# Cross-attention and routed feed-forward on one core: fewer TensorE waits, a split subtraction moved ahead, the last V projection one tile later, and P before rstd in four tiles

## What is computed

```python
x = x + attention(layernorm(x), ctx, ctx, Wq, Wk, Wv, Wo, padding_mask, attention_mask)
x = x + tiled_ffn(layernorm(x), tile_sigs, W, b)
# attention: 16 heads of 32; scores / sqrt(32), masked to -inf, softmax, NaN rows to 0
# tiled_ffn: each position s goes through one of 8 experts:
#   idx = argmax(pe @ sign(tile_sigs).T);  y[b, s] = x[b, s] @ W[idx[s]].T + b[idx[s]]
```

## Time and profile before

| what | value |
|---|---|
| median of three runs | 868.12 us (867.82 to 868.56) |
| the profiled execution's own time | 870.69 us |
| its span, first to last instruction | 868.9 us |
| mean granted TensorE clock | 0.982 of full speed |
| busy share: PE, PE weight loads, DVE, ACT, POOL | 96%, 77%, 81%, 47%, 73% |
| tile loop of the attention | from about 43 us to about 655 us of the span |
| expert stage, PE without a pause | from about 677 us to about 860 us |

### The profile page before, as it was taken

One profiled execution on the slowest core, in us unless ns is written; L12 is line 12 of the kernel. 1 busy time (PEld: TensorE's weight loads), 2 busy tenths in 40 slices (PEclk: granted clock), 3 DMA queues, 4 the chain that ended last, 5 costly groups with the idle time before them and its releaser, 6 DMA issues. The chain is left out here.

```text
span 868.9 us, 25184 instructions
## 1 busy us (share of the span) xinstructions
PE 832.7 (96%) x9583; PEld 669.5 (77%) x9584; DVE 707.6 (81%) x1026; ACT 405.3 (47%) x650; POOL 630.3 (73%) x825
## 2 busy tenths in 40 slices
PE   8999999999999999999999999999883999999996
PEld 6777778778778787887888788777663788888885
DVE  4998898888888888888888888888868877777774
ACT  5545556454654655465555545554555222222221
POOL 3688778786878768776877877686566677777774
PEclk9999999999999999999999999999986999999998
DMA  9522432524253343424344252432578899999992
GB/s 336 197 77 60 152 118 93 159 78 146 75 169 103 112 141 94 150 74 152 100 130 137 84 163 74 136 101 75 174 252 265 251 287 289 300 283 298 294 283 80
DMA packets 123153, 142.08 MB, mean 164 GB/s; under 512 B 16128, under 2 KB 89376, under 8 KB 120992
## 3 DMA queue, kind: packets, MB, share of 16 engines
q1 hardware_dynamic: 108656, 99.45, 36.9%
q0 software_dynamic: 11360, 35.66, 12.7%
q10 hardware_dynamic: 3024, 5.45, 2.0%
HBM read 90.18 MB, written 51.90 MB: 164 GB/s over the span
## 5 line engine op out<-in xcount | busy, mean ns | idle before, releaser
L1818 PE MATMUL banks<-wf_hl,x_hi 128*128 x560 | 139.1, 391 | 1.9 <-DVE wf_hl L356 1.1
L1110 POOL TENSOR_TENSOR s<-s,row 128x1024 f32<-128x1024 f32 x64 | 121.7, 1902 | 3.5 <-DVE row L1360 3.5
L1818 PEld LDWEIGHTS banks<-wf_hl,x_hi 128*128 128x128 f32 x560 | 105.3, 188 | 24.4 <-issue 2.7
L1759 ACT CAST x_hi<-x2t 128x512 fp32r<-128x512 f32 x70 | 43.5, 621 | 148.7 <-PE banks L1818 136.4
L1505 PE MATMUL banks<-wo_hi,ot_hi 128*128 128x512 f32 x256 | 107.8, 421 | 0.0
L1505 PE MATMUL banks<-xt_hi,wq_hi 128*128 128x512 f32 x256 | 105.1, 411 | 0.4 <-ACT vd L1192 0.3
L1086 POOL TENSOR_SCALAR y_mom<-y_mom 128x1 f32<-128x1 f32 x64 | 16.0, 251 | 120.7 <-DVE y_mom L1381 119.5
L1505 PE MATMUL banks<-wo_lo,ot_hi 128*128 128x512 f32 x256 | 101.6, 397 | 0.0
L1505 PE MATMUL banks<-wo_hi,ot_lo 128*128 128x512 f32 x256 | 101.5, 397 | 0.0
L1505 PE MATMUL banks<-xt_hi,wq_lo 128*128 128x512 f32 x256 | 100.5, 392 | 0.0
L1070 POOL TENSOR_TENSOR xt_lo<-xt_raw,xt_hi 128x512 fp32r<-128x512 f32 x64 | 94.4, 1504 | 7.5 <-ACT xt_hi L1177 7.5
(11 more groups left out here) (132 smaller groups left out, 1863.2 us busy)
## 6 DMA issues: line engine op xcount, KB each, us to landing
xq<-x_scratch SPq DMA_DIRECT2D x280, 64.0 KB
xt_raw<-in_x_t SPq DMA_DIRECT2D x16, 1024.0 KB, 6.7
x<-in_x SPq DMA_DIRECT2D x64, 256.0 KB, 3.5
y_scratch<-y_biased SPq DMA_DIRECT2D x64, 256.0 KB, 2.2
x_scratch<-y_normal SPq DMA_DIRECT2D x64, 256.0 KB, 2.9
wf_hl<-in_wf ACTq DMA_DIRECT2D x5, 1024.0 KB, 5.3
ctx_raw<-in_ctx_t SPq DMA_DIRECT2D x32, 128.0 KB, 3.5
wf_hl<-in_wf SPq DMA_DIRECT2D x3, 1024.0 KB, 7.7
```

Source lines behind the costliest of these rows:

```text
L1110: pool.tensor_tensor(p, p, h.row[:, t % h.c, 3, :].unsqueeze(2).broadcast_to([P, H, BK]), ALU.mult)\
L1818: return pe.matmul(pA[:, r % 2, :], rows[:, r % 2, c * P:(c + 1) * P], w, start=first, stop=last)
```

## The change

It has four parts.

1. Waits on TensorE are left out where an earlier wait of the same engine already covers them: in `scores` the ones on `s_drained` (but for t = 1) and `kt_copied`; in `transpose_p` the two on `p_copied` (but for the last tile); in `weigh_v` the one on `ot_lo_ready` and the two on `p_copied` (but for the last two tiles).
2. On POOL, the first piece of wo's low part is put ahead of `normalise_p(0)`, the other three directly behind it, and the wait for `shifted` is dropped.
3. V of the last group is projected in tile 59 and not in tile 58, on TensorE, in ACT's `v_copy` and in the order of the fills.
4. In tiles 59 to 62 POOL does `normalise_p(t + 1)` before `rstd(t + 2)` and not behind it.

```diff
+    def values_at(self, g):
+        return None if g >= self.groups else self.c * g - (1 if g == self.groups - 1 else 2)
...
-            if q == 2 and g + 1 < self.groups:
+            if t == self.values_at(g + 1):
                 names.append(("V", g + 1))
...
+            pool.wait_ge(w_hi_ready["o"], 1)
+            low_of_o(0)
             normalise_p(0)
-            pool.wait_ge(shifted, 2)
-            pool.wait_ge(w_hi_ready["o"], 1)
-            for c in range(KC):
-                ins = pool.tensor_tensor(w_lo["o"][:, c, :], wo_raw[:, c * DM:(c + 1) * DM],
-                                         w_hi["o"][:, c, :].bitcast(F32), ALU.subtract)
+            for c in range(1, KC):
+                ins = low_of_o(c)
             ins.then_inc(w_lo_ready["o"], 1)
...
+                    late = h.tiles - 6 < t < h.tiles - 1
                     if t >= 2:
                         y_rstd(t - 2)
+                    if late:
+                        normalise_p(t + 1)
                     if t + 2 < h.tiles:
                         rstd(t + 2)
...
-                    if t + 1 < h.tiles:
+                    if t + 1 < h.tiles and not late:
                         normalise_p(t + 1)
...
-                    if q == 2 and g + 1 < h.groups:
+                    if t == h.values_at(g + 1):
                         v_copy(g + 1)
...
             def scores(t):
                 g, q = divmod(t, h.c)
-                wait(pe, s_drained, t)
+                if t == 1:
+                    pe.wait_ge(s_drained, t)
                 wait(pe, p_copied, 2 * (t - 1))
                 if q == 0:
-                    pe.wait_ge(kt_copied, g + 1)
                     pe.wait_ge(q_copied, KC * g + KC)
...
                 for b in range(2):
-                    wait(pe, p_copied, 2 * (t - 1) + b + 1)
+                    if t + 1 >= h.tiles:
+                        pe.wait_ge(p_copied, 2 * (t - 1) + b + 1)
...
             def weigh_v(t):
                 g, q = divmod(t, h.c)
-                wait(pe, ot_lo_ready, t)
                 if q == 0:
                     pe.wait_ge(v_copied, g + 1)
                 for c in range(2):
-                    pe.wait_ge(p_copied, 2 * t + c + 1)
+                    if not h.has_scores(t):
+                        pe.wait_ge(p_copied, 2 * t + c + 1)
...
-                    if q == 2 and g + 1 < h.groups:
+                    if t == h.values_at(g + 1):
                         project_v(g + 1)
```

3 lines of the change are left out of this document (added).

## The result

The changed kernel is slower. Its median is 870.50 us (867.67 to 872.85, 9 runs), that of the kernel before, run beside it, 867.99 us (867.33 to 868.56, 9 runs): ratio 1.0027, 95% interval 1.0014 to 1.0040, 1.2 to 3.5 us. The prediction said 866.2 us and a range of 863.7 to 868.6. Both the direction and the range were wrong.

The account below looks back on a forecast made before the run. TensorE, busy 96%, was taken as the bound, with a prologue stall and a ring through DVE and ACT from tile 59. Terms -0.7 - 1.2 + 1.0 - 1.0 = -1.9 gave 866.2 us, range 863.7 to 868.6.

Parts of the forecast that it names:

- Satisfied waits: TensorE, ahead of S, in the transposes and PV: dropping 389 waits that do not hold it changes nothing, 0 us.
- S where it is held: Third tile of each of 15 groups: S starts 0.04 to 0.08 us earlier behind the copies of P, -0.7 us.
- wo's split: Prologue on POOL: P of tile 1 comes 1.9 us earlier, S of tile 3 1.2 earlier, -1.2 us.
- The second rival: Prologue: the split's gain is lost on DVE or POOL, S of tile 3 waits as before; 867.4 us, chance 0.17.
- P ahead of `rstd`: Tiles 59 to 62 on POOL: P starts some 0.4 us earlier, but its transposes are off the ring; zero.
- V one tile on: Tile 59: V's copies on ACT delay the exponential of tile 61, lengthening one ring by 1.2 us; +1.0 us in all.
- the ring: From tile 59 on, the chain from S through DVE and ACT to the next S sets the pace, 8.29 us.
- Clock: Last tiles: V's move removes the first half-clock fall and part of the second; -1.0 us, bounds -3.3 and +2.8.
- The end follows the last tile: Behind tile 63: the expert stage has a fixed length, so whatever moves the last tile moves the end by as much.
- The first (weights loaded ahead): PV in each tile: dropped waits let weights load during the scores, 10 us saved, 856 us; chance 0.04.
- The third: Last tiles: V's copies delay tile 61's exponential, half clock covers S of tile 63 or last output projection; 870.0 us, chance 0.10.
- The fourth: Last tiles: the half-clock falls leave the chain, -3.3 us of clock, 863.9 us; chance 0.20.

Follow-up runs that it names:

- c_split_waits: Kernel before plus wo's split and the dropped waits, V in tile 58, P behind `rstd`: 866.36 us, ratio 0.9987.
- b_split: Kernel before plus wo's low split alone: 865.12 us, ratio 0.9981.
- b_waits: Kernel before with TensorE's satisfied waits dropped and nothing else: 866.72 us, ratio 0.9996.
- d_split_y_first: Kernel before plus wo's split, with ACT's normalisation of y put ahead of the exponential in tiles 59 and 60: 864.49 us, ratio 0.9958.
- e_y_again: The program of d_split_y_first run a second time, against the kernel before: 863.41 us, ratio 0.9949.
- b_v59: Kernel before plus V's move to tile 59 alone: 870.51 us, ratio 1.0039.
- b_p_first: Kernel before plus P ahead of `rstd` in tiles 59 to 62 alone: 866.90 us, ratio 0.9996.

## Why the prediction was wrong

**Satisfied waits, 0.** Right. The earlier trace rows read the price from two changes of shape; 380 more of these waits moved none of those steps.

**S where it is held, -0.7.** Right in mechanism, and in size for this step: 0.10 became 0.05 us in 14 groups (S of tile 4 is not held), 14 x 0.047 = 0.7 us. From S of tile 3 to S of tile 60 the traces show 0.71 (c_split_waits against b_split), 1.06 (b_waits) and 1.65 us less (the change); what makes more than 0.7 is open. Alone the dropped waits are -0.35 us (-1.4 to +0.6), too little for these runs to tell.

**wo's split, -1.2.** Right step by step: the shift of tile 1 prolonged to 1.94 us, P of tile 1 on POOL 2.0 us ahead (1.9 forecast), the shift of tile 2 free again. S of tile 3 came 1.21 us earlier with the split alone, 1.30 with the dropped waits; in time -1.65 us (-2.5 to -0.7). The second rival falls.

**P ahead of `rstd`, 0.** Right. These terms together, -1.9, stand against -1.4 us (-2.3 to -0.6) measured with V back in tile 58.

**V one tile on, +1.0.** Here the prediction failed. The step reads: V's copies "run from 617.7 to 619.2. Behind them in ACT's order stands the exponential of tile 61". It followed what V's move does to V's own copies, and stopped there. But `v_done` has a second reader: the wait ahead of the first expert load, in the same tile 59, ahead of `ot_high`. The order rows showed it, word for word ("waits v_done"), between the two rows that the argument used, and it was not priced. With one more row of ACT before, `ot_high` of tile 59, it could have been:

```profile
614.20 0.59 ACT L1213 CAST ot_hi<-banks 128x512 fp32r<-128x512 f32 x1 [1.75 <-PE banks L1610]
```

V is done 12 matmuls behind 614.7, so at 617.6; `ot_high`, which had run at 614.20, comes behind it at about 618.0; DVE's `ot_low`, maximum and shift end 3.7 us behind that, as before (614.20 to 617.93); the exponential not at 619.2 but at some 621.6; a ring of about 12, and the time on the slower side. Measured: +4.2 us in the ring, +3.4 us (2.3 to 4.5) in time. The part that was priced was too small as well, 1.2 where the load's later place shows 2.01: 0.4 of the difference is the load's own issue (0.39 us), which stands between V and its copies; the other 0.4 is open.

The Trainium skill (Perfetto Trace Analysis, DMA Instruction — HWDGE) describes that an engine's own sequencer waits for the semaphores of a transfer that it issues, and takes its next instruction only after that; its heading names DVE and Sync, and a note has the same mechanism for SP and Activation. The rows agree for ACT: `ot_high` at 613.87 follows the issue of 613.39, and with the issue behind it, it ran at 609.54.

**Clock, -1.0.** This term rested on one execution, and could not carry a number. No run shows it as a gain. The pause ahead of S of tile 62 that V was to fill did not shrink (2.24 us after, 2.06 before), and V left the pause of 1.85 us behind tile 58. There the falls went with the program: all five profiled kernels with V in tile 59 fall to half clock in or just behind that pause, 4.9 to 5.9 us ahead of S of tile 61, and none of the other eleven executions does. In other places the falls do not keep their place from one execution to the next: d_split_y_first and e_y_again are the same program, and one falls at 636.3 us, the other not before 652; and of the sixteen executions only that of before has half clock at 7.5 to 10.9 us, where no kernel differs from another. The prediction took three times within 0.74 us for a sign that the falls keep their place. The rule that it weighed against this (the Trainium skill, TensorE: Matmul & The Clock Gate, Part 1: the activity window is free-running) was the better guide there; by it, the prediction said, the times before should spread by up to 3.3 us. They spread by 1.23 us (9 runs beside the changed kernel), 3.38 and 3.35 (29 runs each), 4.35 (11) and 8.91 (30). How much of that is the clock no run shows.

**The end follows the last tile.** This premise, which stood behind every term, holds only in part: from the last PV to the first expert matmul the executions take 22.2 to 25.3 us, some of it for the transfer of xq.

**The rivals.** The first (weights loaded ahead) falls: PV starts no closer to the scores (147 ns behind their last piece with and without the waits). The third had the right sign and the wrong cause. Its signs came, a pause of 2.08 us ahead of S of tile 63 and half clock from 630.3 us behind it, but not its price: from S of tile 63 to the last PV it takes 14.38 us after and 16.88 before. And undoing V's move alone makes the kernel faster than before. The fourth falls too: 863.9 was not measured, and the falls did not leave the last tiles. What was missing among them is the hold, which needs no clock.

## What to carry to other kernels

When a step is moved later, list *every* reader of its semaphore, not only its own consumer, and for each ask what stands behind that wait in its engine's program order. A wait ahead of a transfer's issue is easy to overlook: the transfer has time, but the engine's queue behind it does not. Filling a pause is safe when the moved instruction comes earlier and its inputs are long ready (the normalisation of y); moved later, it puts its readers at risk. A step that leaves a place can open a pause there. And a difference of clock between two single profiles is no term of a sum.

## What was not expected

- The price of a wait depends on whether the instruction behind it is held: S of a group's first tile started 0.05, 0.10 and 0.21 us behind its last release with two, four and five waits ahead of it, S of tiles 61 to 63 0.05, 0.14 and 0.14 us with one, two and three; satisfied waits elsewhere moved no step by more than 1 ns in the median, doubled or dropped.
- The four profiled executions of b_v59, b_p_first, d_split_y_first and e_y_again have a pause of 1.2 to 1.4 us on TensorE at the same place (in b_v59 at 355.6 us, within a projection of Q), which the trace puts down to issue. None of the eight executions with the dropped waits has it. What causes it was not tried.
